# A long convolution beside linear attention in 35 software-pipelined steps: bank of k's transposes, one counting semaphore, order of the convolution's remainder, of oT's copy and of q's transposes, dtype of the counts

## What is computed

```python
x = x + tanh(g_xattn[0]) * xattn(ctx, ctx, layernorm(x), ssm_kernel, D, 8)
x = x + tanh(g_ffn[0]) * ffn(layernorm(x), conv_w, Wq, Wk, Wv, Wg, router_w, Wout)

# xattn: per head of 8 rows
kv = einsum('bhil,bhjl->bijhl', k, v)              # all pairs i, j of a head
out = causal_conv(kv, ssm_kernel) + kv * D         # over the 512 columns, by FFT
out = einsum('bijhl,bhil->bjhl', out, q)

# ffn: heads H = 16, ratio 2
x = silu(x_prev * conv_w[:, 0] + x * conv_w[:, 1])
q, k, v, g = silu(x @ Wq), x @ Wk, x @ Wv, x @ Wg
q, k = rotary(q), rotary(k)
onehot = one_hot(argmax(logits(v, router_w)))      # one of two experts per position and head
norm = 1 / max(cumsum(onehot), 1)                  # the counts
q_exp, k_exp = q * score * onehot * norm, k * onehot
o = (mask(q_exp @ k_exp.T) * HDK ** -0.5) @ v
out = (silu(g) * layernorm_per_head(o)) @ Wout
```

## Time and profile before

| what | us |
|---|---|
| median of 3 runs | 872.45 |
| the three runs | 872.45, 872.83, 870.46 |
| the profiled execution, its time | 872.01 |
| the profiled execution, its span | 870.2 |
| PE / PEld busy | 826.7 / 691.8 |
| DVE busy | 732.2 |
| POOL busy | 643.6 |
| ACT busy | 438.3 |

### The profile page before, as it was taken

One profiled execution on the slowest core, in us unless ns is written; L12 is line 12 of the kernel. 1 busy time (PEld: TensorE's weight loads), 2 busy tenths in 40 slices (PEclk: granted clock), 3 DMA queues, 4 the chain that ended last, 5 costly groups with the idle time before them and its releaser, 6 DMA issues.

```text
span 870.2 us, 17260 instructions
## 1 busy us (share of the span) xinstructions
PE 826.7 (95%) x6208; PEld 691.8 (80%) x6208; DVE 732.2 (84%) x1489; ACT 438.3 (50%) x941; POOL 643.6 (74%) x579
## 2 busy tenths in 40 slices
PE   3889999999999999999999999999999999999973
PEld 2768888888888888888888888888888888888862
DVE  5798888889888898988889899888888988889842
ACT  3564555555555545545555554555555555554330
POOL 6668778778877787797778778877877887776331
PEclk9798999999999999999999999999999999999996
DMA  8401222012222211222221122222112222210000
GB/s 244 146 3 54 67 68 51 24 60 69 67 68 67 63 26 47 67 69 68 67 68 37 34 66 68 67 68 68 48 25 62 68 68 67 68 50 13 2 14 23
DMA packets 26676, 51.78 MB, mean 59 GB/s; under 512 B 3232, under 2 KB 4640, under 8 KB 26592
## 3 DMA queue, kind: packets, MB, share of 16 engines
q1 hardware_dynamic: 22320, 46.19, 19.5%
q10 hardware_dynamic: 4272, 4.48, 1.6%
HBM read 42.12 MB, written 8.55 MB: 58 GB/s over the span
## 4 chain that ended last, share of the span: by engine, by line
PE 87%; issue 3%; POOL 1%; DVE 1%; POOLq 0%; ACT 0%; DVEq 0%; ACTq 0%
PE bank L333 39%; PE bank L304 25%; PE bank L285 10%; PE bank L370 4%; PE bank L385 4%; PE bank L317 2%; PE bank L293 2%; PE bank L320 1%; PE bank L443 0%; POOL rstd L710 0%; POOLq L68 0%; POOL o_rstd L710 0%; DVE y_raw L848 0%; POOL rot_b L739 0%; DVE x L992 0%
## 5 line engine op out<-in xcount | busy, mean ns | idle before, releaser
L304 PE MATMUL bank<-kv_pair,toep 128*128 128x512 f32 x960 | 244.8, 401 | 1.0 <-DVE z_terms L838 1.0
L304 PEld LDWEIGHTS bank<-kv_pair,toep 128*128 128x128 f32 x960 | 175.3, 190 | 41.0 <-DVE z_terms L838 7.5
L704 POOL TENSOR_TENSOR kv_pair<-kv,kv_pair 128x576 fp32r<-128x576 f32 x126 | 178.1, 1425 | 6.2 <-ACT kv_pair L536 2.8
L695 POOL TENSOR_TENSOR kv<-kx 128x512 f32<-128x512 f32 x128 | 160.5, 1254 | 5.5 <-DMA kx<-in_ctx 4.1
L710 POOL TENSOR_TENSOR o_rstd<-o_ve,minus_half 128x16 f32<-128x16 f32 x32 | 93.2, 2911 | 78.4 <-DVE o_ve L924 78.4
L848 DVE TENSOR_REDUCE y_raw<-z_terms 128x128 f32<-128x1024 f32 x128 | 149.2, 1204 | 0.0
L710 POOL TENSOR_TENSOR rstd<-ve,minus_half 128x1 f32<-128x1 f32 x64 | 39.2, 612 | 120.3 <-DVE ve L1003 117.3
L333 PE MATMUL bank<-w_all_high,yT_high 128*128 128x512 f32 (+2 forms) x512 | 119.6, 355 | 0.0
L333 PE MATMUL bank<-w_all_low,yT_high 128*128 128x512 f32 (+2 forms) x512 | 111.7, 340 | 0.0
L333 PE MATMUL bank<-w_all_high,yT_low 128*128 128x512 f32 (+2 forms) x512 | 106.1, 339 | 0.0
L536 ACT ACTIVATE kv_pair<-kv 128x576 fp32r<-128x576 f32 x128 | 87.2, 682 | 20.6 <-POOL kv L698 19.7
(11 more groups left out here) (108 smaller groups left out, 1517.5 us busy)
## 6 DMA issues: line engine op xcount, KB each, us to landing
toep<-taps_dram SPq DMA_DIRECT2D x31, 512.0 KB, 7.0
kx<-in_ctx SPq DMA_DIRECT2D x32, 384.0 KB, 7.5
x_in<-in_x SPq DMA_DIRECT2D x32, 256.0 KB
out_x<-out_sb SPq DMA_DIRECT2D x32, 256.0 KB
wv_t<-in_L_ffn_Wv ACTq DMA_DIRECT2D x1, 1024.0 KB, 8.5
w_g<-in_L_ffn_Wg ACTq DMA_DIRECT2D x1, 1024.0 KB, 6.9
w_out<-in_L_ffn_Wout ACTq DMA_DIRECT2D x1, 1024.0 KB, 9.9
w_qk<-in_L_ffn_Wq ACTq DMA_DIRECT2D x1, 512.0 KB, 4.6
```

Source lines behind the costliest of these rows:

```text
L304: ins = nc.tensor.matmul(bank[lc % 2][:, :], toep[:, 1 - p, a, (lc - mc) * P:(lc - mc + 1) * P], kv_p[b][:, 1 - p, mc, 0:FULL], start=(mc ...
L695: eng.tensor_tensor(view(kv[:, c % 2, 0:FULL], [[ROW, NROT], [1, ROW]]), view(kx[:, p, c, 0:ROW], [[0, NROT], [1, ROW]]), view(kx[:, p, c, ...
L704: eng.tensor_tensor(kv_p[1][:, p, c, :], kv[:, c % 2, :], kv_p[0][:, p, c, :].bitcast(F32), ALU.subtract).then_inc(kv_ready[c], 1)
```

## The change

- k's transposes go to bank 4 (v's bank) instead of bank 7, behind a wait for v_copied instead of gatedT_ready; ACT copies keT from bank 4. The waits of the z and gated transposes on bank 7 name other semaphores.
- The four semaphores mask_done0..3 become one, `masked`, which counts; attention_output waits for it once, and its wait for v_copied is dropped, as are three waits ahead of scores.
- `conv_last` stands ahead of attention_output instead of behind the transposes of oT; at h = -1 it stays behind `conv` 2.
- ACT copies oT behind the two Silus instead of ahead of the second kv_round.
- q's transposes stand behind v's projection, and ACT's `extend` of q behind the copies of v and gatedT.
- rank and u are float32r: rank has a tile of its own, loaded by an own DMA and rounded by ACT at h = -1; constants are laid out in another order. Its wait on s_gates rises from 48 to 64.

```diff
@@ constants and tiles
-        const = sb("const", C_COLS)
+        const = sb("const", C_COLS - P)
+        rank = stack.enter_context(nc.sbuf_tensor("rank", [P, P], F32R))
-        u = sb("u", 2, RH)
+        u = stack.enter_context(nc.sbuf_tensor("u", [P, 2, RH], F32R))
-        mask_done = [sem(f"mask_done{i}") for i in range(CH)]
+        masked = sem("masked")
+
+        def mask_count(r, h1):
+            return CH * (h1 - 1) + r + 1
@@ PE
                 def attention_output():
-                    for r in range(CH):
-                        eng.wait_ge(mask_done[r], h)
-                    eng.wait_ge(v_copied, h)
+                    eng.wait_ge(masked, mask_count(CH - 1, h))
...
                 def scores():
-                    eng.wait_ge(qeT_sb, h + 1)
                     eng.wait_ge(keT_sb, h + 1)
-                    eng.wait_ge(gate_ready, h + 1)
                     if front:
                         eng.wait_ge(x2_ready, h + 2)
-                    eng.wait_ge(v_copied, h + 1)
...
+                if front and h != -1:
+                    if can_wait(h):
+                        eng.wait_ge(masked, mask_count(0, h))
+                    else:
+                        eng.wait_ge(x2_ready, h + 1)
+                    conv_last(p, h + 1)
                 if tail:
                     attention_output()
                 if front:
                     eng.wait_ge(mul_done[0], h + 2)
                     conv(p, 2, h + 1)
+                if h == -1:
+                    conv_last(p, h + 1)
                 if tail:
                     eng.wait_ge(oT_sb, h)
                     transpose4(bank[4], lambda c: oT[:, c, :], o_ps)
-                if front:
-                    if can_wait(h):
-                        eng.wait_ge(mask_done[0], h)
-                    elif can_wait(h + 1):
-                        eng.wait_ge(x2_ready, h + 1)
-                    conv_last(p, h + 1)
...
-                    nc.tensor.matmul(bank[6][:, 0:RH], rank, u[:, 0, :], start=True, stop=True).then_inc(cnt_ps, 1)
+                    nc.tensor.matmul(bank[6][:, 0:RH], rank[:, :], u[:, 0, :], start=True, stop=True).then_inc(cnt_ps, 1)
+                if back:
+                    if can_wait(h):
+                        eng.wait_ge(o_gated, h)
+                    project(bank[4], yT_p, w_all_p, V0, DV, v_ps, y_low, h + 1)
                 if pre and h != -1:
                     eng.wait_ge(qn_ready, h + 3)
                     if front:
                         eng.wait_ge(mul_last, h + 2)
                     transpose4(bank[2], lambda c: qn[:, c * P:(c + 1) * P], qT_ps)
-                if back:
-                    if can_wait(h):
-                        eng.wait_ge(o_gated, h)
-                    project(bank[4], yT_p, w_all_p, V0, DV, v_ps, y_low, h + 1)
...
-                    if tail:
-                        eng.wait_ge(gatedT_ready, h)
-                    transpose4(bank[7], lambda c: qke[:, RH + 4 * c:RH + 4 * c + 4, :, :], keT_ps)
+                    eng.wait_ge(v_copied, h + 1)
+                    transpose4(bank[4], lambda c: qke[:, RH + 4 * c:RH + 4 * c + 4, :, :], keT_ps)
@@ ACT
-                if tail:
-                    eng.wait_ge(oT_ps, h)
-                    if can_wait(h - 1):
-                        eng.wait_ge(o_ps, h - 1)
-                    eng.activation(oT[:, :, :], bank[4][:, :].rearrange("p (c n) -> p c n", c=CH), ACT.Copy
-                                   ).then_inc(oT_sb, 1)
                 if pre:
                     kv_round(p, 1, h + 2)
...
                     eng.activation(y_raw[:, :, :], y_raw[:, :, :], ACT.Silu).then_inc(y_ready, 1)
+                if tail:
+                    eng.wait_ge(oT_ps, h)
+                    if can_wait(h - 1):
+                        eng.wait_ge(o_ps, h - 1)
+                    eng.activation(oT[:, :, :], bank[4][:, :].rearrange("p (c n) -> p c n", c=CH), ACT.Copy
+                                   ).then_inc(oT_sb, 1)
...
                     if h == -1:
-                        eng.wait_ge(s_gates, 48)
+                        eng.wait_ge(s_gates, 64)
+                        eng.activation(rank[:, :], x2[:, 3, 0:P], ACT.Copy)
...
                     if first_step:
+                        eng.dma_start(x2[:, 3, 0:P], consts[:, C_RANK:C_RANK + P]).then_inc(s_gates, 16)
...
+                if pre and h >= 0:
+                    extend_q(p, h)
```

More of the change, by code:

```diff
@@ L16 @@
 EPS = 1e-5
-C_ID, C_MASK, C_RANK, C_COS, C_SIN, C_COLS = 0, 128, 256, 384, 400, 416
+C_ID, C_MASK, C_COS, C_SIN, C_RANK, C_COLS = 0, 128, 256, 272, 288, 416
 C_ANTI, C_CENTRE, C_IND, C_END = 416, 544, 672, 676
@@ L166, in flamingo_gated_layer @@
         mask = const[:, C_MASK:C_MASK + P]
-        rank = const[:, C_RANK:C_RANK + P]
         s_taps_in, s_taps_out, s_consts, s_gates, s_wv, s_wqk, s_wg, s_wout = (
@@ L391, in step @@
                     eng.wait_ge(z_ready, h + 1)
-                    if can_wait(h):
-                        eng.wait_ge(keT_sb, h)
+                    if h == 0:
+                        eng.wait_ge(logit_low, 1)
+                    elif h == 1:
+                        eng.wait_ge(y_conv, h)
                     else:
-                        eng.wait_ge(logit_low, 1)
+                        eng.wait_ge(gatedT_ready, h - 1)
                     transpose4(bank[7], lambda c: z[:, c * P:(c + 1) * P], zT_ps)
@@ L429, in step @@
                     if can_wait(h):
-                        eng.wait_ge(mask_done[3], h)
+                        eng.wait_ge(masked, mask_count(3, h))
                     project(bank[3], yT_p, w_all_p, 0, DK, q_ps, y_low, h + 1, passes=(0, 1))
@@ L463, in step @@
                     if can_wait(h):
-                        eng.wait_ge(mask_done[2], h)
+                        eng.wait_ge(masked, mask_count(2, h))
                     if h == 0:
@@ L528, in extend, with extend_q @@
                 eng.activation(dst[:, :, ROW:EXT], psum[:, :, 0:EXT - ROW], ACT.Copy).then_inc(done, 1)
+            def extend_q(p, h):
+                eng.wait_ge(qT_ps, h + 3)
+                if can_wait(h + 1):
+                    eng.wait_ge(mul_last, h + 1)
+                    eng.wait_ge(mul_done[CH - 1], h + 1)
+                extend(qx[:, p, :, :], bank[0 if h == -1 else 2], qx_ready)
             def kv_round(p, c, h2):
@@ L625, in step @@
                         kv_round(p, 3, h + 2)
-                    eng.wait_ge(qT_ps, h + 3)
-                    if can_wait(h + 1):
-                        eng.wait_ge(mul_last, h + 1)
-                        eng.wait_ge(mul_done[CH - 1], h + 1)
-                    extend(qx[:, p, :, :], bank[0 if h == -1 else 2], qx_ready)
+                    if h < 0:
+                        extend_q(p, h)
                     if first_step:
+                        eng.dma_start(x2[:, 3, 0:P], consts[:, C_RANK:C_RANK + P]).then_inc(s_gates, 16)
                         eng.dma_start(w_conv[:, :, :], conv_w.rearrange("(c p) k -> p c k", p=P)).then_inc(s_gates, 16)
@@ L662, in step @@
                     eng.wait_ge(keT_ps, h + 1)
-                    eng.activation(keT[:, :, :], bank[7][:, :].rearrange("p (c n) -> p c n", c=CH), ACT.Copy
+                    eng.activation(keT[:, :, :], bank[4][:, :].rearrange("p (c n) -> p c n", c=CH), ACT.Copy
                                    ).then_inc(keT_sb, 1)
@@ L1041, in shape_constants @@
     centre = np.eye(P) - heads @ heads.T / HDV
-    parts = [np.eye(P), same * HDK ** -0.5 / 2, rank, cos, cos, -sin, sin, np.eye(P)[:, ::-1], centre, heads]
+    parts = [np.eye(P), same * HDK ** -0.5 / 2, cos, cos, -sin, sin, rank, np.eye(P)[:, ::-1], centre, heads]
     return np.concatenate([a.astype(np.float32) for a in parts], axis=1)
```

9 lines of the change are left out of this document (4 added, 5 removed).

## The result

The changed kernel takes 890.51 us (median of 4 runs, 890.08 to 892.46) where the kernel before takes 872.08 (4 runs): a ratio of 1.021, 95% interval 1.020 to 1.022. It is slower by 18.4 us. The profiled execution has a time of 890.89 us and a span of 889.1.

A forecast was written before the change was run, and what follows sets the result against it. PE bounds the kernel, a DVE dependency loop nearly as long; 13.46 + 12.42 gives 25.88 us per step against 25.20. 0.8 + 19.0 + 0.3 + 0.65 = 20.8 on 872.01 gives 892.8, lowered to 892.0; range 876 to 904.

The forecast's parts named there:

- the semaphore's 0.13: At attention output, one wait instead of five saves PE 0.13 us per step, bounds 0 and 0.49.
- the end of the kernel: In the drain, step 31, the later oT copy adds 0.84 us; output waits give -0.13, counts -0.06: 0.65.
- The slack of 0.07 us: DVE's work from oT's transposes to qke's signed copy takes 13.46 us with a semaphore, beside PE's 13.53.
- the first part: PE's stretch from the end of oT's transposes to qke's first transpose load: 13.53 us before, 13.46 forecast.
- The second part: PE's stretch from qke's first transpose load to the next end of oT's transposes: 11.67 us before, 12.42 forecast.
- Counts: On PE, one matmul of counts instead of two saves 0.06 us per step, bounds 0 and 0.14.
- k's bank: k's transposes in bank 4 no longer wait for gatedT's low part: 0.12 us saved per step, bounds 0 and 0.16.
- q's order 0: q's transposes behind v are the same matmuls in another order: cost 0, a late qn stays hidden.
- the copy of oT hidden by 0.14: ACT's copy behind the two Silus ends at 454.52, semaphore included; PE wants it at 454.66, so it costs nothing.
- DVE idle ahead of o_var: A sign: DVE idles some 1.3 us before o_var in every step, a wait absent from the earlier trace.
- Waits at the counts 0.3, at the sums and qke 0.75: PE waits 1.05 us per step for DVE: about 0.3 at the counts, some 0.75 at the transposes of sums and qke.
- The rival with POOL's lock: DVE's o_rstd product escapes overlap with POOL's rotation, shortening DVE's work to 12.47 us; kernel faster at 864; chance 0.12.

The follow-up runs named there:

- The two experiments that shorten the chain: DVE's norm of x moved ahead of y's low part, x loaded one step earlier: on the changed kernel 861.69 us; with remainder and oT copy moved back, 862.06.
- the version without these waits: The changed kernel with DVE's norm of x ahead of the low part of y and x loaded one step earlier: 861.69 us.
- a 0.6 us addition: The kernel before with one superfluous DVE statistic of x_in behind multiply 2: 950.0 us, ratio 1.088.
- three other kernels: Superfluous DVE statistic ahead of qke's signed copy in the kernel before (892.97 us) and the changed kernel (909.91); ahead of y's low part in the kernel before (877.05).

## Why the prediction was right

Forecast 892.0, measured 890.5: the mechanism holds, and so do nearly all sizes, two of them by luck (the semaphore's 0.13, and the end of the kernel).

- **The slack of 0.07 us.** Right, and the deciding number. The chain stayed at 13.40 and the first part fell from 13.53 to 13.45 (worked out: 13.46). The two experiments that shorten the chain show both sides of it.
- **The second part**, forecast 12.42, measured 12.33. By the ends of the matmuls the remainder takes 1.00 there, as said. The attention output and the convolution behind it gave 0.17 instead of 0.13, and the stretch of qke's transposes 0.18 instead of 0.12: the load there starts behind a wait, with nothing of PE's ahead of it. In the version with the norm and its load moved, where that wait is gone, the stretch gives 0.12. The prediction had named this effect, at up to 0.05 a step, and set its forecast 0.8 us under its sum for it (up to 1.4 less for the effect, 0.44 more for the median over the profiled execution). So the period is 25.78 instead of 25.88: the term that was mis-sized by 0.1 is the second part's savings.
- **One semaphore**, 0.13. Alone it gave 0.15. But the working gave the wrong reason for what remains, and in the changed kernel the gain isn't the semaphore's. It read the 0.35 without a load at the scores as the price of the change of shape, and promised that gap at the output. After, there is none: the last load of the remainder ends at 460.42 and the output's first starts at 460.46. What the loads waited for in before was the 512-column matmul in front of them, which the remainder's 64-column one has replaced. By ends, the output's first product comes 0.35 behind the matmul before it in before, 0.23 with one semaphore, 0.23 in the changed kernel and 0.23 with the remainder alone and four semaphores too. With the remainder ahead the waits are over in time anyhow (DVE's last mask ends 1.10 ahead of the load); there the semaphore brings nothing of its own, and that the sum fits at this term is luck. The Trainium skill's page "TensorEngine Tiling (Array Packing)", section "Key Properties", has a drain at a change of the tiling mode: the 0.23, against the 0.08 of the 64-column matmul just ahead of it, would fit, but a load gap doesn't measure it.
- **Counts** 0.06, measured 0.07 together with q's order. **k's bank** 0.12, measured 0.09 alone.
- **q's order 0, the copy of oT hidden by 0.14.** Right in this kernel: the copy ends 0.16 ahead of the load, 0.11 with the 0.05 for a semaphore that the forecast's 0.14 had taken off. What the prediction missed is that both are tied to the remainder. Without the q edit there is a wait of 0.47 for qn (under the chain), and without the remainder the late copy costs 0.68.
- **DVE idle ahead of o_var**, promised 1.3, measured 0.85. The low part of y takes 1.21 us instead of 0.77 (the row of L926 above), since it now runs beside POOL's product of kv_pair (460.69 to 463.53 in that step), with both its inputs in SBUF. It is off the chain and changed nothing.
- **Waits at the counts 0.3, at the sums and qke 0.75.** Measured 0.35, then 0.40 and 0.46 (10.7 / 27, 12.4 / 27). Together 1.21 of waiting loads; by the version without these waits they cost 1.01 a step, 13.45 - 12.37 = 1.08 of it in the first part, where the prediction had 1.05. The second part gets 0.07 of that back (12.33 against 12.40) by the effect told above.
- **The ends.** The first oT ends 0.95 later (forecast 0.87); the 29 periods behind it add 16.7 us (forecast 29 x 0.68 = 19.7); from there to the end it is 1.2 (the forecast's 20.8 leave 0.2). The whole is 18.9 instead of 20.8: 3.0 too many in the periods stand against 1.0 too few behind them, and that they partly cancel is luck. Some 0.8 of the 1.2 wasn't foreseen: the last four matmuls ran at 1.00 (2.4 GHz) in before and at 0.50 (1.2 GHz) in after (columns as in the earlier trace rows, before, then after):

```profile
860.00:864.00 4.00, 3.69 (x9) 2.92 (x10) 0.69 (x1) 0.26 (x1) 0.00 (x0) 0.50 0.00 0
864.00:866.00 2.00, 1.03 (x5) 0.51 (x3) 0.75 (x1) 0.00 (x0) 0.00 (x0) 1.00 0.00 0
```

```profile
878.00:882.00 4.00, 3.60 (x9) 2.83 (x10) 0.69 (x1) 0.35 (x1) 0.00 (x0) 0.50 0.00 0
882.00:884.00 2.00, 1.88 (x5) 0.97 (x3) 0.08 (x1) 0.00 (x0) 0.00 (x0) 0.50 0.00 0
```

In both kernels PE came out of an idle stretch of 5.34 us ahead of gated's transposes, and was busy 3.6 to 3.7 of 4 us at the lower level; in before the clock rose at 864.0, in time for these matmuls, in after at 884.2, behind the last of them. Why not sooner, these runs don't show.

- **The rival with POOL's lock** (chance 0.12) didn't come: the product with o_rstd is 1679 ns at the median. But its mechanism is real, and it is how the norm's move pays. There the product starts ahead of rot_a and takes 693 ns, while the signed copy, now beside POOL's kv, takes 1408 instead of 676 (ns, all steps):

```profile
L968 DVE TENSOR_TENSOR gated<-gated,o_rstd x32: 693/693/1761, 82.2 to 846.5; 128x512 f32<-128x512 f32 x32
...
L870 DVE SCALAR_TENSOR_TENSOR qke<-qke,u x32: 670/1408/1408, 61.4 to 829.4; 128x512 f32<-128x512 f32 x32
```

From o_var to the signed copy that is 1.12 us less: the norm's 1.07 and the product's 0.99 gone, 0.73 added by the copy, and some 0.2 of waiting for o_rstd.

Of the edits, the semaphore and k's bank are small gains at the remainder's old place, and so are the counts, which were measured only together with q's order; the version with these and with both moves taken back (862.45), and the one with all edits and the norm of x moved with its load (861.69), both beat the kernel before by over 1%. They can't be told apart, and what they do brings nothing more together (862.06).

## What to carry to other kernels

When an instruction is moved, ask first what its old place covered: here 1 us of PE work had been the cover of a chain on another engine with 0.07 us to spare, and moving it cost nearly its whole length although no work was added. Cut the period at the two points where the engines meet, compare the chain with the work beside it, and take the slack as the number that decides. Edits that fill or need the same cover must be costed together, and an edit that seems to cost nothing may do so only because of another.

## What the runs showed of the hardware

- A DVE product of 128x256 with two SBUF inputs took 0.42 us when it started as little as 0.02 us ahead of POOL's rotation, and 1.36 or 1.52 when it started 0.22 behind rot_a or 0.26 behind rot_b. That made a 0.6 us addition cost 2.67 us per step. In three other kernels it struck in a single step, in which DVE was 0.35 late, and cost 1.10 of the 1.45 lost there. The length of such a chain is no constant: it depends on its phase against POOL.
- Overlap with a POOL product took the low part of y from 0.77 to 1.21 us and the signed copy from 0.68 to 1.41.
- A gap without weight loads ahead of the attention output was mostly the large matmul in front: with one semaphore 0.36 us behind 512 columns, 0.04 behind 64.
- Idle time between PE's rows understated what waits cost: 0.46 us a step idle, 1.01 lost.
- Five waits in a row on PE (four masks and v), against one, cost 0.13 to 0.15 us a step where the last mask was done 0.23 us ahead of the load, and nothing where it had been done for 1.10 us.
